# A transformer block over 32 batches: eight batches per turn of the hardware loop instead of four

## The chip, the cores and the metric

One NeuronCore of a Trainium2 chip runs the kernel. The metric is device time in microseconds (us), the median of the runs of one program. Its engines are TensorE (PE; its weight loads are shown as PEld), VectorE (DVE), ScalarE (ACT), GpSimd (POOL) and SyncE (SP), which here issues the transfers. They run their own instruction streams and wait for each other on semaphores.

## The reference

For x of shape 32 x 256 x 128, each batch goes through attention with 16 heads of 8, then two layer norms and a linear layer:

```python
y = layernorm(x, ln_w, ln_b)
q, k, v = y @ wq, y @ wk, y @ wv              # per head, 8 wide
w = softmax(q @ k.T / sqrt(8) + causal)       # 256 x 256, per head
x1 = norm(2 * x + concat(w @ v) @ wo)         # norm: no weights, eps 1e-5
W_eff = W + up_aux @ (lora_up @ (lora_down @ down_aux))
out = norm(x1 + x1 @ W_eff.T + b)
```

All data is float32; the weights are the same for all batches.

## The kernel before

One batch is the unit of work, and all batches are alike. The kernel is a software pipeline over iterations `it` from -4 to 34. An iteration does the parts of several batches at once: stage by stage, the part with offset `o` works on batch `it + o` (offset 4 and 3: statistics of x, normalising, q, k, v and their split into bf16 parts; 2: the transfers that spread the heads, `expand`; 1: row maxima; 0 and -1: scores, exp, masks, weights times v; -1 and -2: output projection and the first norm; -3: linear layer, the last norm and the store). Tiles that live across iterations are rings of 4, so an iteration's tiles are known from its number modulo 4.

Within an iteration the order on each engine is written out by hand in 16 steps `s`. TensorE does up to one unit of row-maxima matmuls (`max_scores`, lines 635 to 640) and one head's scores (lines 652 and 653) in each, with the other matmuls in `side`. VectorE reduces each unit (`row_max`, line 527), with two PSUM banks between the two engines. ScalarE takes the exp of the scores (line 460) and, once per iteration in step 2, copies the transposed maxima into `mT` (line 407); this instruction is a good mark of the iteration. SyncE then writes `mT` into rows of the scores' operand (`qx<-mT`, `max_rows`, line 269), and the first scores of that batch wait for it (line 652). GpSimd masks the exponentials (line 351) and does the small work of the norms. Between engines everything goes by semaphores that only count up; there is no barrier at a turn of the loop.

The instruction stream of each engine is made by `iterate`: iterations -4 to 3 as straight code, a hardware loop over iterations 4 to 23 with four of them in its body (five turns), and iterations 24 to 34 as straight code again. The loop closes with a compare-and-branch on each engine by itself. In the loop the counts that waits compare with are registers, made by `done` through `snap`; in straight code they are constants.

Of the kernel before, what the change touches and what calls it, by code (L numbers as in the profile page):

```python
# [12 lines left out]
BATCHES, SEQ, D = 32, 256, 128  # L13
# [18 lines left out]
RING = 4  # L32
FIRST, LAST = -4, BATCHES + 2
LOOP_FROM = RING
LOOP_TO = LOOP_FROM + (BATCHES - 5 - LOOP_FROM) // RING * RING
RANK, DDIM, UDIM = 4, 100, 50


# [63 lines left out]
def iterate(eng, step):  # L102

    for it in range(FIRST, LOOP_FROM):
        step(Iteration(eng, it, 0, {}))
    with eng.Fori(LOOP_FROM, LOOP_TO - RING + 1, RING) as base:
        cache = {}
        for u in range(RING):
            step(Iteration(eng, base, u, cache))
    for it in range(LOOP_TO, LAST + 1):  # L110
        step(Iteration(eng, it, 0, {}))


def build(nc, x, ln_w, ln_b, wq, wk, wv, wo, w_t, bias, down_t, up_t, down_aux, up_aux_t, out):
    with ExitStack() as ctx:  # L115
# [121 lines left out]
        def _(sp):  # L237
# [34 lines left out]
            def step(it):  # L272
# [19 lines left out]
                if it.runs(3):  # L292
# [3 lines left out]
                    store_parts()  # L296

            iterate(sp, step)
            sp.wait_ge(s_st, 16 * BATCHES)

        @block.gpsimd
        def _(pool):
# [95 lines left out]

            make_masks()
            iterate(pool, step)  # L400

        @block.scalar
        def _(act):
# [60 lines left out]
            for tile, dram in first_weights:  # L464
# [6 lines left out]
                           ACT.Copy).then_inc(s_kmask, 1)  # L471
            act.wait_ge(s_w1, N_W1)
            iterate(act, step)

        @block.vector
# [318 lines left out]
```

## Time and profile before

| | |
|---|---|
| median of 3 runs | 531.74 us |
| the runs | 530.07, 531.74, 531.96 us |
| profiled execution | 532.91 us, of which span 531.1 us |
| mean granted TensorE clock | 0.958 of full speed |
| instructions in the trace | 15,978 |

The span reaches from the first to the last instruction; 1.8 us of the profiled execution lie outside of it. The tables of the profile count only the work of an engine: register, branch and semaphore instructions are left out of busy time and of the counts. "issue" as the end of a wait means that the profile shows nothing that the engine waited for. Queues that the transfer view calls "instruction" carry program code to the engines.

### The profile page before, as it was taken

How to read it: one execution, taken by the hardware profiler on the slowest of the kernel's cores; microseconds unless marked ns; L12 is line 12 of the kernel's file. 1: busy time of each engine (PE TensorE's matmuls, PEld its weight loads, DVE VectorE, ACT ScalarE, POOL GpSimd, SP SyncE). 2: the span in 40 equal slices, each digit the busy share in tenths (PEclk: the TensorE clock that was granted, in tenths of full speed). 3: DMA queues.
4: the chain of work that ended last, by engine and by line, in shares of the span. 5: the costliest groups of instructions: out<-in, count | busy, mean ns of one | idle time of the engine just before them, and what ended most of it. 6: DMA issues, size and time to landing. Idle time of an engine off the chain costs nothing. (4 is left out here: it accounts for less than half of the span.)

```text
span 531.1 us, 15978 instructions
## 1 busy us (share of the span) xinstructions
PE 456.2 (86%) x5512; PEld 333.4 (63%) x5512; DVE 405.9 (76%) x1071; ACT 338.6 (64%) x803; POOL 392.5 (74%) x571
## 2 busy tenths in 40 slices
PE   2467699999899999999999999999999999989861
PEld 1245466767676776676767676676677676666431
DVE  1487778888888888888888888888888888888332
ACT  4212477677776777677767777777767777767620
POOL 6543666888788888888887888888888888866543
PEclk9995799999999999999999999999999999999875
DMA  2554366656655555556665665555555665650000
GB/s 62 139 139 122 87 130 151 162 144 146 157 141 149 145 145 148 138 144 159 160 160 126 156 154 152 138 142 147 147 146 142 162 162 141 128 148 23 23 20 20
DMA packets 70857, 69.11 MB, mean 130 GB/s; under 512 B 6955, under 2 KB 66146, under 8 KB 66146
## 3 DMA queue, kind: packets, MB, share of 16 engines
q1 hardware_dynamic: 70242, 68.48, 52.4%
q8 instruction: 22, 0.36, 0.3%
q10 hardware_dynamic: 576, 0.13, 0.1%
q14 instruction: 17, 0.14, 0.1%
HBM read 47.07 MB, written 20.99 MB: 128 GB/s over the span
## 5 line engine op out<-in xcount | busy, mean ns | idle before, releaser
L527 DVE TENSOR_REDUCE rowmax<-max_bank 128x2 f32<-128x512 f32 (+1 forms) x384 | 253.6, 682 | 46.5 <-PE max_bank L635 31.3
L460 ACT ACTIVATE probs<-score_bank 128x384 f32<-128x384 f32 x512 | 232.1, 491 | 60.0 <-PE score_bank L653 51.3
L351 POOL TENSOR_SCALAR_AFFINE_SELECT probs<-probs 128x1024 f32<-128x1024 f32 x128 | 140.5, 1098 | 40.7 <-ACT probs L460 37.0
L652 PE MATMUL score_bank<-qx,kx 74*128 74x256 bf16 x512 | 133.5, 276 | 5.8 <-DMA qx<-mT 3.5
L639 PE MATMUL max_bank<-kx,qx 128*128 128x128 bf16 x512 | 89.7, 227 | 23.1 <-DVE rowmax L527 21.5
L653 PE MATMUL score_bank<-qx,kx 74*128 74x128 bf16 x512 | 108.7, 220 | 0.0
L668 PE MATMUL pv_bank<-probs,v_ext 128*32 128x256 f32 (+1 forms) x2048 | 105.5, 335 | 2.9 <-POOL probs L351 2.9
L640 PE MATMUL max_bank<-kx,qx 74*128 74x128 bf16 x512 | 89.2, 226 | 0.0
L668 PEld LDWEIGHTS pv_bank<-probs,v_ext 128*32 128x32 f32 x2048 | 55.9, 110 | 42.4 <-issue 17.7
L639 PEld LDWEIGHTS max_bank<-kx,qx 128*128 128x128 bf16 x512 | 48.3, 100 | 51.6 <-DVE rowmax L527 45.1
L338 POOL TENSOR_TENSOR rs<-ve,power 128x2 f32<-128x2 f32 x96 | 69.3, 722 | 8.0
L395 POOL TENSOR_TENSOR parts<-rest,parts 128x512 bf16<-128x512 f32 x32 | 39.6, 1238 | 40.4 <-ACT parts L439 40.4
L635 PE MATMUL max_bank<-kx,qx 128*128 128x128 bf16 x512 | 52.0, 226 | 11.6 <-DVE rowmax L527 6.8
L652 PEld LDWEIGHTS score_bank<-qx,kx 74*128 74x128 bf16 x512 | 50.4, 98 | 14.9 <-ACT probs L460 8.0
L342 POOL TENSOR_SCALAR y<-f,mv,rs 128x128 f32<-128x128 f32 x64 | 51.0, 806 | 8.7 <-POOL rs L338 8.7
L342 POOL TENSOR_SCALAR xhat<-xa,mv,rs 128x128 f32<-128x128 f32 x64 | 51.0, 805 | 8.3 <-POOL rs L338 8.3
L640 PEld LDWEIGHTS max_bank<-kx,qx 74*128 74x128 bf16 x512 | 51.4, 100 | 1.0
L653 PEld LDWEIGHTS score_bank<-qx,kx 74*128 74x128 bf16 x512 | 50.3, 98 | 0.8
L635 PEld LDWEIGHTS max_bank<-kx,qx 128*128 128x128 bf16 x512 | 31.5, 99 | 28.6 <-issue 18.3
L433 ACT ACTIVATE parts<-bank 128x512 bf16<-128x512 f32 x32 | 19.1, 597 | 41.6 <-PE bank L723 41.6
L575 DVE TENSOR_TENSOR rest<-bank,parts 128x512 f32<-128x512 f32 x32 | 22.1, 692 | 28.6 <-ACT parts L433 28.6
L413 ACT ACTIVATE pv_s<-pv_bank 128x256 f32<-128x256 f32 x64 | 24.6, 384 | 26.6 <-PE pv_bank L668 25.3
(76 smaller groups left out, 612.1 us busy)
## 6 DMA issues: line engine op xcount, KB each, us to landing
kx<-k_rows SPq DMA_DIRECT2D x96, 192.0 KB
qx<-q_rows SPq DMA_DIRECT2D x64, 192.0 KB
qx<-q_rows SPq DMA_DIRECT2D x32, 208.0 KB
q_rows<-parts SPq DMA_DIRECT2D x32, 192.0 KB, 2.1
k_rows<-parts SPq DMA_DIRECT2D x32, 192.0 KB, 2.4
xa<-in_x SPq DMA_DIRECT2D x32, 128.0 KB, 5.6
k_rows<-parts SPq DMA_DIRECT2D x32, 128.0 KB, 2.2
xr<-in_x SPq DMA_DIRECT2D x32, 128.0 KB, 6.5
```

The source lines that it names most:

```text
L338: pool.tensor_tensor(rs[:, :], ve[:, :], power[:, :], ALU.pow).then_inc(signal, 1)
L342: ins = pool.tensor_scalar(to[:, n, :], source[:, n, :], mv[:, n, 0:1], rs[:, n:n + 1], ALU.subtract, ALU.mult)
L351: pool.affine_select(out=t, in_=t, compare_op=ALU.is_ge, fill=0.0, base=0, pattern=[[0, GROUP * NB], [1, P]], channel_multiplier=-1)\
L395: pool.tensor_tensor(parts[:, 2, :, :], rest[:, :, :], parts[:, 1, :, :], ALU.subtract).then_inc(s_p3, 1)
L460: act.activation(probs[:, h, 0:PW], score_bank[SCORE_BANK[h]][:, 0:PW], ACT.Exp, scale=SCALE / Q_SCALE)\
L527: dve.tensor_reduce(to, of, AX.X, ALU.max).then_inc(s_mread[unit], 1)
L635: ins = pe.matmul(b[:, g * P:g * P + P], q[:, h, 0:P], k[:, h, 0:P], start=True, stop=True)
L639: pe.matmul(b[:, g * SEQ:g * SEQ + P], q[:, h, P:SEQ], k[:, h, P:SEQ], start=True, stop=True)
L640: ins = pe.matmul(b[:, g * SEQ + P:g * SEQ + SEQ], q[0:SCORE_ROWS, h, P:SEQ], k[0:SCORE_ROWS, h, 0:P], start=True, stop=True)
L652: pe.matmul(b[:, 0:SEQ], k[0:SCORE_ROWS, i, 0:P], q[0:SCORE_ROWS, i, :], start=True, stop=True)
L653: pe.matmul(b[:, SEQ:PW], k[0:SCORE_ROWS, i, P:SEQ], q[0:SCORE_ROWS, i, P:SEQ], start=True, stop=True).then_inc(s_score[h], 1)
L668: ins = pe.matmul(pv_bank[VW * g:VW * g + VW, n * P:SEQ], v_ext[r][:, n, head(h), window], probs[:, h, 0:SEQ] if n == 0 else probs[:, h, S ...
```

## The change

`TURN`, twice the ring, takes the place of `RING` as the loop's step and as the number of iterations in its body. `LOOP_TO` is 4 + 23 // 8 * 8 = 20 instead of 4 + 23 // 4 * 4 = 24. So the loop covers iterations 4 to 19 in two turns of eight, and the straight code behind it iterations 20 to 34. The rings stay at 4 tiles, and nothing changes in what an iteration does or in its order.

```diff
 LOOP_FROM = RING
-LOOP_TO = LOOP_FROM + (BATCHES - 5 - LOOP_FROM) // RING * RING
+TURN = 2 * RING
+LOOP_TO = LOOP_FROM + (BATCHES - 5 - LOOP_FROM) // TURN * TURN
...
     for it in range(FIRST, LOOP_FROM):
         step(Iteration(eng, it, 0, {}))
-    with eng.Fori(LOOP_FROM, LOOP_TO - RING + 1, RING) as base:
+    with eng.Fori(LOOP_FROM, LOOP_TO - TURN + 1, TURN) as base:
         cache = {}
-        for u in range(RING):
+        for u in range(TURN):
             step(Iteration(eng, base, u, cache))
     for it in range(LOOP_TO, LAST + 1):
         step(Iteration(eng, it, 0, {}))
```

## Rows read from the trace of the kernel before

**Rows 1.** The page, part 1: busy us, share of the span, instructions.

```profile
PE 456.2 (86%) x5512; PEld 333.4 (63%) x5512; DVE 405.9 (76%) x1071; ACT 338.6 (64%) x803; POOL 392.5 (74%) x571
```

**Rows 2.** Grouped waits, whole span: us in total, times, longest us.

```profile
ACT probs L460 <- PE score_bank L653: 51.3, 104, 3.6
PEld max_bank L639 <- DVE rowmax L527: 45.1, 98, 1.3
...
DVE rowmax L527 <- PE max_bank L635: 31.3, 38, 1.1
```

**Rows 3.** In order of time, ScalarE, batches 4, 8, 9, 12, 16, 20, 24, 26, 28: start, us.

```profile
106.10 0.37 ACT L407 ACTIVATE mT<-bank 32x256 bf16<-32x256 bf16 x1
...
164.31 0.37 ACT L407 ACTIVATE mT<-bank 32x256 bf16<-32x256 bf16 x1
...
178.59 0.37 ACT L407 ACTIVATE mT<-bank 32x256 bf16<-32x256 bf16 x1
...
221.94 0.37 ACT L407 ACTIVATE mT<-bank 32x256 bf16<-32x256 bf16 x1
...
279.57 0.37 ACT L407 ACTIVATE mT<-bank 32x256 bf16<-32x256 bf16 x1
...
337.20 0.37 ACT L407 ACTIVATE mT<-bank 32x256 bf16<-32x256 bf16 x1
...
394.40 0.37 ACT L407 ACTIVATE mT<-bank 32x256 bf16<-32x256 bf16 x1
...
422.95 0.37 ACT L407 ACTIVATE mT<-bank 32x256 bf16<-32x256 bf16 x1
...
451.65 0.37 ACT L407 ACTIVATE mT<-bank 32x256 bf16<-32x256 bf16 x1
```

**Rows 4.** In order of time: TensorE and VectorE at a turn's boundary, TensorE mid-turn.

```profile
161.11 0.23 PEld L635 LDWEIGHTS max_bank<-kx,qx 128*128 128x128 bf16 x4 [0.38 <-issue]
...
163.24 0.10 PEld L639 LDWEIGHTS max_bank<-kx,qx 128*128 128x128 bf16 x1 [0.89 <-DVE rowmax L527]
...
162.49 0.69 DVE L527 TENSOR_REDUCE rowmax<-max_bank 128x4 f32<-128x512 f32 x1 [0.49 <-issue]
...
204.32 0.23 PEld L635 LDWEIGHTS max_bank<-kx,qx 128*128 128x128 bf16 x4 [0.20 <-issue]
...
206.06 0.10 PEld L639 LDWEIGHTS max_bank<-kx,qx 128*128 128x128 bf16 x1 [0.50 <-DVE rowmax L527]
```

**Rows 5.** Transfer queues (packets, MB, share): 100 to 165, 165 to 390, 390 to 531.

```profile
q8 instruction: 6, 0.10, 0.6%
q14 instruction: 5, 0.04, 0.2%
...
DMA packets 33280, 33.38 MB, mean 148 GB/s; under 512 B 3140, under 2 KB 30944, under 8 KB 30944
## 3 DMA queue, kind: packets, MB, share of 16 engines
q1 hardware_dynamic: 33280, 33.38, 60.6%
...
q8 instruction: 11, 0.18, 0.6%
q14 instruction: 8, 0.07, 0.1%
```

**Rows 6.** Busy time (x instructions) of the loop's second turn, by engine.

```profile
160.30:217.90 57.60, 54.03 (x692) 39.96 (x688) 48.41 (x133) 41.46 (x101) 47.38 (x69) 1.00 0.61 149
```

**Rows 7.** First turn, 135 to 139.5: q8's packet, the landing of qx<-mT, TensorE's wait.

```profile
q8 instruction: 1, 0.02, 1.3%
...
DMA to landing us min/median/max: 1.8/2.7/3.6
...
139.25 0.10 PEld L652 LDWEIGHTS score_bank<-qx,kx 74*128 74x128 bf16 x1 [1.37 <-DMA qx<-mT]
```

**Rows 8.** The page, part 6: transfers, KB each, median us from issue to landing.

```profile
xr<-in_x SPq DMA_DIRECT2D x32, 128.0 KB, 6.5
...
qx<-mT SPq DMA_DIRECT2D x64, 8.0 KB, 1.9
```

## The prediction

> **What bounds the kernel now.** I read the page's busy shares first, then the grouped waits, then the instructions in order of time at one turn boundary, and last the instruction transfers. The reader should see in the shares that no engine is full: TensorE 86% by the modelled matmuls, its weight loads 63%, VectorE 76%, GpSimd 74%, ScalarE 64% [rows 1]. The engines take turns. The waits say it: TensorE waits 45 us for the row maxima of VectorE, VectorE 31 us for the maxima's scores, ScalarE 51 us for scores [rows 2]. So a batch is a chain through several engines, and a delay of any of them can reach the end, less what slack there is.
>
> The period is very regular. Inside a turn of the loop two successive batches are 178.59 - 164.31 = 14.28 us apart. In the straight part behind the loop they are 422.95 - 408.68 = 14.27 us apart. A whole turn of four, with its boundary, takes 279.57 - 221.94 = 57.63 us, and the next 337.20 - 279.57 = 57.63 us [rows 3]. Four batches by themselves are 4 x 14.27 = 57.08 us. So a taken turn boundary costs 0.55 us, and a batch in the loop costs what a batch in straight code costs. At the last turn, where the branch falls through, 394.40 - 337.20 = 57.20 us: 0.12 us.
>
> The 0.55 us can be seen at 160 to 163 us: after the branch TensorE stands 0.38 us for "issue" ahead of its first maxima matmul, where the same place in the middle of a turn shows 0.20; VectorE stands 0.49 us for "issue"; TensorE then waits 0.89 us for VectorE, where it waits 0.50 in the middle of a turn [rows 4].
>
> **The change, part by part.** The operations on data are the same. The loop now covers batches 4 to 19 in two turns of eight, and 20 to 23 move to the straight part.
>
> (a) Boundaries. Before: four taken, one falling through. After: one taken (behind batch 11), one falling through (behind 19). Removed: 3 x 0.55 = 1.65 us. As the boundary shows as lost time in the period itself, nothing hides it, and the whole 1.65 comes off. The batches that move into straight code bring 0, since both kinds take 14.27. The register work ahead of each batch is hidden in either form. Bounds: 1.65 is what rows show; it can't be more than the total of 4 x 0.55 + 0.12 = 2.3 us.
>
> (b) Instructions no longer stay. The instruction transfers tell where code comes from. From 100 to 165 us, the loop's first turn, the queue q8 brings 6 packets (0.10 MB, 16 KB each) and q14 brings 5 of 8 KB. From 165 to 390 us, turns two to five, there is no instruction packet at all. From 390 us on there are 11 and 8 again [rows 5]. So the body of four batches was fetched once and stayed in the engines' instruction memories. TensorE runs 692 matmuls and as many weight loads in a turn [rows 6]; 6 packets of 16 KB over those 1,384 are about 71 bytes each, with its waits and register instructions in the rest, so q8 is TensorE's. After the change its body is twice that: some 2,770 such instructions, 12 packets, 190 KB. Whether this stays, no row shows; the rows show only that some 96 to 112 KB did. I take it that it doesn't: the head of the body has been overwritten when the branch goes back to it, and TensorE stops until its block comes. VectorE and ScalarE also double, and may stop at the same boundary.
>
> The Trainium skill (Advanced Engine Details and Errata, ISA Cache) gives TensorE 128 KB of it, the others 32 KB, in 256-instruction lines. By that page the old body fits, which agrees with the empty stretch of 225 us, and the new one does not. Another of its rules stands with rival 3.
>
> The price of such a stop. One q8 packet is 1.3% of 16 engines in 4.5 us, 0.94 us [rows 7]. From issue to landing the small transfer qx<-mT takes 1.9 us [rows 8]. Request, way and packet together: 1.9 + 1.0 = 2.9 us on TensorE. The trace has one stop of known net price. At 137.9 us TensorE stands 1.37 us for qx<-mT [rows 7], and this first turn takes 164.31 - 106.10 = 58.21 us [rows 3], 0.58 over the others, so some 0.8 us of the stop were absorbed. Net: 2.9 - 0.8 = 2.1 us. VectorE and ScalarE stop in the same microseconds (VectorE's first instruction behind the branch is at 162.5, TensorE's at 161.1 [rows 4]), so their stops lie beside TensorE's and are counted at 0; if VectorE's came after TensorE's, in series, it would cost another 2 to 3 us. Bounds: below, 0 (the block is there after all); above, 6.5 us, the landing of the xr read in this traffic [rows 8], less 0.8, 5.7 us. I take 2.1, near the small transfers, as the block is one packet.
>
> (c) Refetching collides. During the fetches of the first turn one packet of q8 falls into the landing of qx<-mT, the maxima rows that the next scores wait for: it lands after 3.6 us instead of 1.8 [rows 7], and TensorE stands. The small transfer is issued once per batch, a 16 KB fetch comes about every 10 us, so their places shift from batch to batch. The price of four batches with fetches is 0.58 us in the first turn and (451.65 - 394.40) - 57.08 = 0.17 us in batches 24 to 27 [rows 3]. Fetching batches grow by 16: 8 to 11 in the first turn, all eight of the second, 20 to 23 in straight code. The first four of the second turn are the code of the first turn's first four: 0.58. The other twelve at 0.17 per four: 0.51. Sum 1.1 us. Bounds 4 x 0.17 = 0.7 and 4 x 0.58 = 2.3 us.
>
> Sum: -1.65 + 2.1 + 1.1 = +1.55 us. Against the profiled execution's own 532.91 us (span 531.1 and 1.8 around it) this is 534.5. That execution lies 1.2 us above the median of the runs shown, 531.74, so the median to expect is 531.74 + 1.55 = 533.3 us, 0.3% slower.
>
> **The rivals.** A change under 0.5% (2.7 us) can't be told from none here.
>
> Rival 1, the body stays, or its head is fetched ahead in time. For it: no fetch in 225 us of loop, and no limit of the memory is shown. Then (b) is 0 and of (c) only batches 8 to 11 and 20 to 23 pay, 2 x 0.17 = 0.34: -1.65 + 0.34 = -1.3, 530.4 us. Against: twice the code. Chance 0.13.
>
> Rival 2, the other side: the stops come in series. VectorE's head block returns later than TensorE's, or a block just behind the head has gone too and is missed in turn. Two stops of 2.9 less 0.8 are 5.0: -1.65 + 5.0 + 1.1 = +4.45, 536.2 us, 0.8% slower. It decides from a net stop above 2.66 + 1.65 - 1.1 = 3.2 us. For it: VectorE's branch comes over a microsecond behind TensorE's, and the DMA engines are 60% busy. Against: only one boundary is taken, and no other fetch shows as a stop of its own. Chance 0.23.
>
> Rival 3, each taken boundary of the old loop already contains a fetch, so that its price stays as it is. Then (b) is 0 with (c) full: -1.65 + 1.1 = -0.55, 531.2 us. Against it: no instruction packet from 165 to 390 us, with four boundaries taken in the loop, three of them in that stretch [rows 5]. Chance 0.04. It would be the rule of the Trainium skill (Runtime: NRT & Kernel Launch, Instruction fetch mechanics) that a taken branch outside the current two pages always forces a fetch; the trace contradicts it for this loop, whose TensorE body is six packets long.
>
> **How the numbers follow.** My forecast, one stop with most of it net, 530.8 to 534.9 us around 533.3, has 0.60. Rivals 1 to 3 have 0.13, 0.23 and 0.04. The range is 530.5 to 536.3: low end rival 1, high end rival 2; outside it are a stop near the upper bound and noise of the runs (1.9 us between those shown). Slower by over 0.5%: rival 2, 0.23, and a little of the forecast's upper tail, 0.25 together. Faster by over 0.5% would need more than all of the 2.3 us that boundaries cost, and could only come from the spread of runs: 0.03. Within 0.5%: 0.72.
>
> **What the profile after would show.** For (a): batches at 14.27 us, with one excess instead of four. For (b): instruction packets all through the second turn, and behind batch 11 a stand of 2 to 4 us on TensorE put down to "issue", with VectorE's beside it; that batch takes some 17 us instead of 14.88. For (c): packets on q8 growing from 22 to about 34, and now and then a landing of qx<-mT over 3 us with a wait on line 652. The prediction is wrong if the second turn has no instruction packets (rival 1), or if the boundary behind batch 11 costs over 4 us or has a second stop close behind it (rival 2).

## The result and the profile after

The changed kernel takes 535.5 us, the median of 7 runs (534.06 to 536.09), against 531.74 us before (7 runs, 530.07 to 532.67). The ratio is 1.0071, with a 95% interval from 1.0051 to 1.0092: slower, by about 0.7%. The time lies in the predicted range of 530.5 to 536.3, but not where the likeliest case had it (533.3, within 0.5%). Ratios here and below leave out runs more than 1.5% above the fastest of their kernel, which are four of the six of experiment 4 and one of the ten of experiment 10.

In order of time, ScalarE's copy into mT marks batches 4, 8, 11, 12, 13, 14 and 28 (start, us), as in [rows 3]:

```profile
105.99 0.37 ACT L408 ACTIVATE mT<-bank 32x256 bf16<-32x256 bf16 x1
...
163.23 0.37 ACT L408 ACTIVATE mT<-bank 32x256 bf16<-32x256 bf16 x1
...
206.43 0.37 ACT L408 ACTIVATE mT<-bank 32x256 bf16<-32x256 bf16 x1
...
225.36 0.37 ACT L408 ACTIVATE mT<-bank 32x256 bf16<-32x256 bf16 x1 [0.24 <-PE bank L683]
...
241.87 0.37 ACT L408 ACTIVATE mT<-bank 32x256 bf16<-32x256 bf16 x1
...
256.16 0.37 ACT L408 ACTIVATE mT<-bank 32x256 bf16<-32x256 bf16 x1
...
456.83 0.37 ACT L408 ACTIVATE mT<-bank 32x256 bf16<-32x256 bf16 x1
```

Batch 13 to 14 takes 14.29 us, the old period. From 11 to 12, over the only taken boundary, it is 18.93 us, and from 12 to 13 again 16.51 us. Together 35.44 - 2 x 14.27 = 6.90 us for one boundary that used to cost 0.55. The same microseconds in order of time, the first instruction behind the branch on three engines (start, us, and in brackets the idle time before it):

```profile
221.20 0.35 PEld L636 LDWEIGHTS max_bank<-kx,qx 128*128 128x128 bf16 x4 [3.42 <-issue]
...
222.14 0.69 DVE L528 TENSOR_REDUCE rowmax<-max_bank 128x4 f32<-128x512 f32 x1 [3.09 <-PE max_bank L636]
...
222.24 0.49 ACT L461 ACTIVATE probs<-score_bank 128x384 f32<-128x384 f32 x1 [4.04 <-PE score_bank L654]
```

TensorE stands 3.42 us for nothing that the profile shows, where [rows 4] have 0.38. The records of the branch itself say more (engine, operation, duration in ns three times, start). First the kernel before at the same boundary, then the one after, then the code packets from 217.3 to 221.1 us of the one after:

```profile
L106 PEldq COMPARE_BRANCH  x1: 220/220/220, 217.9 to 217.9; - x1
```

```profile
L107 PEldq COMPARE_BRANCH  x1: 3627/3627/3627, 217.3 to 217.3; - x1
...
L107 DVEq COMPARE_BRANCH  x1: 74/74/74, 218.9 to 218.9; - x1
...
L107 ACTq FUSED_REGOPS  x1: 35/35/35, 219.7 to 219.7; - x1
...
L107 DVEq FUSED_REGOPS  x1: 51/51/51, 221.9 to 221.9; - x1
```

```profile
q14 instruction: 3, 0.02, 2.2%
q8 instruction: 1, 0.02, 2.0%
```

The stop is TensorE's branch, which lasts 3.63 us instead of 0.22, and one 16 KB packet of its code moves meanwhile. Before, no code packet moves there. The register operation is the first instruction behind a branch. VectorE's comes at 221.9, three microseconds after its branch, and ScalarE's at 219.7, 2.6 us after its branch at 217.1, where the kernel before has some 0.3 us on each. So these two have a stop of their own beside TensorE's, and TensorE's late matmuls hide its end: when they go on, they have no input yet. The queues of program code (packets, MB, share of 16 engines), 165 to 225 us and 225 to 340 us:

```profile
q8 instruction: 7, 0.11, 0.8%
q14 instruction: 8, 0.07, 0.4%
...
q8 instruction: 11, 0.18, 0.7%
q14 instruction: 5, 0.04, 0.1%
```

There is code traffic all through the second turn, where [rows 5] show none in a loop turn after the first. What the prediction did not have is in the busy time by stretch (us, PE busy and its matmuls, granted clock, DMA share, GB/s):

```profile
210.00:220.00 10.00, 7.70 (x98) 1.00 0.70 178
220.00:230.20 10.20, 8.99 (x65) 0.50 0.32 84
230.20:240.20 10.00, 9.51 (x123) 1.00 0.54 130
```

From late in the stop on, TensorE's granted clock is 0.50, 1.2 GHz, for 10.2 us: it is busy 8.99 us for 65 matmuls, where ten microseconds at 2.4 GHz hold 123.

The books between the two profiled executions. From batch 4 to batch 28 the old one takes 451.65 - 106.10 = 345.55 us [rows 3], which is 3.07 over 24 x 14.27; the new one takes 350.84, 8.36 over. Of the 8.36, 6.90 are the one boundary, 1.46 the falling-through one and the fetches. Of the 3.07, 2.3 are boundaries. So 5.3 us are lost there, and the spans differ by only 3.3 (534.4 against 531.1). The rest is in the drain of the pipeline: behind batch 28 the old execution needs 79.45 us and the new one 77.57. The old one shows a granted clock of 0.51 in one stretch there that the new one has at full speed. First the kernel before, then the one after:

```profile
499.80:503.30 3.50, 3.41 (x25) 0.51 0.02 5
```

```profile
499.80:513.50 13.70, 9.59 (x125) 1.00 0.11 32
```

This part varies from one execution to another of any of these kernels. In all twelve profiled executions the clock stays at half at the very end, from 507 to 533 us on. Six of them have one more stretch at half clock in the drain, with full clock behind it again (before and experiments 2, 3, 7, 9, 10), and need 79.0 to 79.8 us behind batch 28. The six without it (after and experiments 1, 4, 5, 6, 8) need 77.3 to 78.0 us. The medians differ by 3.8 us; how many of the other runs had the stretch is not on record.

### The profile page after: what moved, and what is told of

Read it like the earlier page. It is cut to its first block and busy times, and to the rows that moved or that the text cites. A ratio compares the mean times of both kernels' runs of the same rounds, so it can differ in the third digit from the quotient of the medians.

```text
span 534.4 us, 15820 instructions
## 1 busy us (share of the span) xinstructions
PE 458.9 (86%) x5512; PEld 336.0 (63%) x5512; DVE 406.4 (76%) x1071; ACT 338.1 (63%) x803; POOL 391.4 (73%) x571
## 5 line engine op out<-in xcount | busy, mean ns | idle before, releaser
L640 PE MATMUL max_bank<-kx,qx 128*128 128x128 bf16 x512 | 90.5, 228 | 19.8 <-DVE rowmax L528 17.9
L636 PE MATMUL max_bank<-kx,qx 128*128 128x128 bf16 x512 | 52.7, 228 | 15.5 <-DVE rowmax L528 6.8
```

Of the source, the lines that this page charges most:

```text
L636: ins = pe.matmul(b[:, g * P:g * P + P], q[:, h, 0:P], k[:, h, 0:P], start=True, stop=True)
L640: pe.matmul(b[:, g * SEQ:g * SEQ + P], q[:, h, P:SEQ], k[:, h, P:SEQ], start=True, stop=True)
```

## The experiments

All were timed beside runs of the kernel before on the same chip, which had medians of 530.6 to 531.0 us. Line numbers in their rows are those of the experiment's own file. "Late" is what the two batches over the boundary, 11 to 12 and 12 to 13, take over 2 x 14.28 us in the profiled execution. The kernel before is itself 0.6 us late there (14.88 and 14.28).

**1. The old body, boundaries as after.** Two turns of four, then straight code from batch 12 on.

```diff
-LOOP_TO = LOOP_FROM + (BATCHES - 5 - LOOP_FROM) // RING * RING
+LOOP_TO = LOOP_FROM + 2 * RING
```

> Boundaries as in the changed kernel (one taken, one falling through), but the body keeps four batches; more straight code than in either. Theory 1 (TensorE's head block is gone at the boundary of the body of eight; it stops 3.6 us and its clock falls to half): no stop and no clock drop here, branch 0.25 us as before, three boundaries fewer (-1.65) against up to +1.1 for refetching: 0.5 to 1.5 us faster than before, about 530.5. Theory 2 (the loss is spread over all batches that fetch their code): as in the changed kernel, 2 to 4 us slower than before.

530.16 us, ratio 0.9993 (0.9970 to 1.0015): no different from before. Much more code is fetched here than before and nearly as much as in the changed kernel (39 packets on q8 and 28 on q14, against 22 and 17 before and 46 and 35 after), and nothing is lost. Theory 2, a loss spread over all fetching batches, falls. The expected gain is not resolved in the medians. In the profiled executions, from batch 4 to batch 28, it can be seen: 450.19 - 105.81 = 344.38 us, against 345.55 before.

**2 and 3. The long body on TensorE alone, and on all but TensorE.** Each engine makes its own loop, so the number of batches per turn can differ between them.

```diff
+    turn = 2 * RING if eng.engine == mybir.EngineType.PE else RING       # 2
+    turn = RING if eng.engine == mybir.EngineType.PE else 2 * RING       # 3
+    loop_to = LOOP_FROM + (BATCHES - 5 - LOOP_FROM) // turn * turn
...
-    with eng.Fori(LOOP_FROM, LOOP_TO - RING + 1, RING) as base:
+    with eng.Fori(LOOP_FROM, loop_to - turn + 1, turn) as base:
```

> Only TensorE has the body of eight and two turns; the other engines keep four and five turns. Theory 1: TensorE's branch behind batch 11 again takes some 3.6 us with half clock after it, boundary about 6.9 us, the other engines' own boundaries stay hidden or cost up to 0.5 each: 535 to 537 us. Theory 3 (VectorE's and ScalarE's missing blocks set the stop): near before, within 1.5 us, and no half clock.

> TensorE keeps four batches and five turns, the other four engines have eight. Theory 1: no stop of TensorE at its branches; stops of the others for their 8 KB blocks at most 1 to 2 us once, no half clock: within 1.5 us of before. Theory 3: 3 us or more slower than before.

TensorE alone: 537.43 us, ratio 1.0103 (1.0075 to 1.0131). All but TensorE: 535.42 us, ratio 1.0077 (1.0052 to 1.0101). Either half of the change by itself loses what the whole does. Experiment 2 went as theory 1 had it, 0.4 us above the expected time. Experiment 3 did not: theory 1, with TensorE as the only culprit, is wrong, and theory 3, with the others as the only one, is wrong by experiment 2. The two also show whose queue is whose: from 165 to 390 us experiment 2 has 23 packets on q8 and none on q14, experiment 3 has 17 on q14 and none on q8. The stop of experiment 2 in order of time, then the instructions of experiment 3 at the same place:

```profile
222.03 0.23 PEld L637 LDWEIGHTS max_bank<-kx,qx 128*128 128x128 bf16 x4 [3.74 <-issue]
```

```profile
218.54 0.25 DVE L508 BATCH_NORM_AGGREGATE mv<-st 128x2 f32<-128x6 f32 x2
222.27 1.29 DVE L529 TENSOR_REDUCE rowmax<-max_bank 128x4 f32<-128x512 f32 x2 [3.48 <-issue]
...
219.49 0.87 ACT L462 ACTIVATE probs<-score_bank 128x384 f32<-128x384 f32 x2 [1.56 <-issue]
...
223.02 0.23 PE L641 MATMUL max_bank<-kx,qx 128*128 128x128 bf16 x1 [3.78 <-DVE rowmax L529]
```

In experiment 3 it is VectorE that stands for "issue", 3.48 us, ScalarE 1.56 us, and TensorE's matmuls wait 3.78 us for VectorE (its weight loads 4.00). Its clock falls all the same, though its own body of four stayed and its own branch behind batch 11 took 0.22 us. Experiment 3's busy time by stretch, columns as above:

```profile
219.20:223.00 3.80, 0.04 (x1) 1.00 0.31 86
223.40:226.80 3.40, 3.40 (x31) 0.51 0.03 7
226.80:236.80 10.00, 9.51 (x125) 1.00 0.62 160
```

**4. A prefetch hint for the branch**, on the changed kernel.

```diff
-    with eng.Fori(LOOP_FROM, LOOP_TO - TURN + 1, TURN) as base:
+    with eng.bass.Fori(LOOP_FROM, LOOP_TO - TURN + 1, TURN, engines=[eng.engine], hint_back_edge=True) as base:
```

> The changed kernel with a prefetch hint for the loop-closing branch as the first instruction of each turn. Theory 1: the head block is on hand, TensorE's branch falls from 3.6 us to a few tenths, no half clock behind it; 6.3 us of the boundary come back, 529 to 530 us, 1.5 to 2.5 us faster than before. Theory 2: no faster than the changed kernel, 535. If the hint doesn't reach the block either, the branch stays at 3.6 us.

551.76 us is the median of six runs (541.07 to 554.95). The ratio, 1.0264 (1.0197 to 1.0331), is of two of them alone, 541.07 and 548.98 us: the worst kernel of the study, by an amount that is loosely known. The profiled execution took 554.95 us, so only its stops are read here, not its time. In order of time:

```profile
223.37 0.34 PEld L636 LDWEIGHTS max_bank<-kx,qx 128*128 128x128 bf16 x4 [3.67 <-issue]
...
357.09 0.29 DVE L538 TENSOR_TENSOR attn<-bank,rden 128x128 f32<-128x128 f32 x1 [6.92 <-issue]
...
396.32 0.38 ACT L414 ACTIVATE pv_s<-pv_bank 128x256 f32<-128x256 f32 x1 [6.50 <-issue]
```

TensorE's stop stayed. From 165 to 345 us the queue of the other engines' code is empty, where the changed kernel had 13 packets from 165 to 340. But behind the loop two new stops of 6.9 and 6.5 us appear, on VectorE and ScalarE, in straight code. My expectation was wrong. Why the hint does nothing for TensorE, and why the others then stop twice as long, is open.

**5. No loop at all.**

```diff
-    for it in range(FIRST, LOOP_FROM):
+    for it in range(FIRST, LAST + 1):
         step(Iteration(eng, it, 0, {}))
-    with eng.Fori(LOOP_FROM, LOOP_TO - RING + 1, RING) as base:
...
-    for it in range(LOOP_TO, LAST + 1):
-        step(Iteration(eng, it, 0, {}))
```

> All iterations straight, no boundary at all, every batch fetches its code. Boundaries: -(4 x 0.55 + 0.12) = -2.3 us. Theory 1 (the loss of the changed kernel is the one stop at the taken boundary): no stop, refetching up to +0.1 per batch for 20 batches, so between -2.3 and 0: 528.5 to 530.5 against 530.6 of before. Theory 2 (fetching code costs in itself): slower than before by 1 us or more.

529.5 us, ratio 0.9987 (0.9964 to 1.0009): inside what theory 1 expected, but not told apart from before. From batch 4 to batch 24 it takes 391.48 - 105.52 = 285.96 us, 0.4 over 20 x 14.28, all of it with code being fetched:

```profile
105.52 0.37 ACT L401 ACTIVATE mT<-bank 32x256 bf16<-32x256 bf16 x1
...
391.48 0.37 ACT L401 ACTIVATE mT<-bank 32x256 bf16<-32x256 bf16 x1
```

**6 and 7. Which of the others.** The edit is that of 2 and 3, with VectorE alone, and with GpSimd and SyncE, at eight.

> Only VectorE has the body of eight. Theory 4 (each engine whose doubled body outgrows its instruction memory stops some 3.3 us at the taken branch, and any one of VectorE and TensorE is enough): VectorE's gap behind its branch is 3.3 us as with all four, TensorE starves, its clock falls for a while, batches 11 and 12 take 5 us too much: 534 to 536. If ScalarE or SyncE made the stop: near before.

> Only GpSimd and SyncE have bodies of eight: some 246 and 214 instructions of their own streams, against 368 of VectorE, 322 of ScalarE and 2,878 of TensorE. Theory 4: both bodies stay, no stop, no instruction packets for them in the second turn, within 1 us of before. If every doubled body is lost: a stop of 3 us on GpSimd, 2 to 4 us slower.

VectorE alone: 535.62 us, ratio 1.0086 (1.0056 to 1.0115), the same stop again. GpSimd and SyncE: 529.73 us, ratio 0.9980 (0.9961 to 0.9999), no loss, and from 195 to 345 us, which holds its second turn, no packet of code. Experiment 6 in order of time with the records around VectorE's branch, then all of experiment 7's transfers from 195 to 345 us, where only the data queue moves anything:

```profile
222.41 1.29 DVE L529 TENSOR_REDUCE rowmax<-max_bank 128x4 f32<-128x512 f32 x2 [3.50 <-issue]
...
223.16 0.10 PEld L641 LDWEIGHTS max_bank<-kx,qx 128*128 128x128 bf16 x1 [4.02 <-DVE rowmax L529]
```

```profile
L108 DVEq COMPARE_BRANCH  x1: 74/74/74, 218.8 to 218.8; - x1
...
L108 DVEq FUSED_REGOPS  x1: 51/51/51, 222.1 to 222.1; - x1
```

```profile
DMA packets 22081, 22.36 MB, mean 149 GB/s; under 512 B 2073, under 2 KB 20505, under 8 KB 20505
...
q1 hardware_dynamic: 22081, 22.36, 60.0%
```

Theory 4 holds: each engine's own body decides. All instructions counted, waits and registers too, GpSimd's 246 and SyncE's 214 stay; VectorE's 368 and TensorE's 2,878 don't. ScalarE's 322 stop for 1.56 us in experiment 3, beside VectorE's stop; no run has ScalarE alone at eight, and none has a body length between these, so the limit of no engine is known.

**8 and 9. A stop without a taken branch.** Experiment 1 with a reduction on VectorE that nobody reads, once, ahead of batch 12's first row maximum, in straight code. It adds work and changes no output. The loop's branch falls through just ahead of it, and from 217 to 225 us one 8 KB packet of code moves; both are so in experiment 1 too, which is 0.2 us late (14.45 and 14.28).

```diff
             def step(it):
+                if it.static and it.base == 12:
+                    dve.wait_ge(s_pause, 1)
+                    dve.tensor_reduce(pause_to[:, :], pause[:, :], AX.X, ALU.max)
                 for s in range(HEADS):
```

> The kernel with two turns of four, and in the straight code ahead of batch 12's first row maximum one reduction over 128 x 3072 on VectorE that nobody needs (about 3.3 us). No fetch, no branch there. Theory 5 (a stop costs its length and, because TensorE starves, a stretch at half clock): TensorE waits some 3.5 us for VectorE, its clock falls to 1.2 GHz, batches 11 and 12 take 4.5 to 5.5 us too much: 534.5 to 535.5. If the half clock or the second late batch came with the fetching: 2.5 to 3 us too much and the clock stays: 533.

> As the kernel with the pause of 3.35 us, but the reduction is over 128 x 1536, some 1.75 us. Theory 5: the pause passes to TensorE, less 0.5 to 0.9 us of slack. If the half clock needs the long stop, batches 11 and 12 take only 0.9 to 1.4 us too much and the granted clock stays at 2.4 GHz: 530.5 to 531.5. If any pause of this kind lowers it: 2.5 us or more too much, near 533.

3.35 us of pause: 535.68 us, ratio 1.0109 (1.0076 to 1.0143), as slow as the change. 1.75 us: 533.22 us, ratio 1.0034 (1.0006 to 1.0062). In order of time and by stretch (columns as above), the long pause:

```profile
219.91 3.35 DVE L602 TENSOR_REDUCE pause_to<-pause 128x1 f32<-128x3072 f32 x1
...
223.91 0.10 PEld L645 LDWEIGHTS max_bank<-kx,qx 128*128 128x128 bf16 x1 [3.82 <-DVE rowmax L530]
```

```profile
224.80:228.30 3.50, 3.50 (x33) 0.51 0.16 33
```

and the short one:

```profile
219.22 1.75 DVE L602 TENSOR_REDUCE pause_to<-pause 128x1 f32<-128x1536 f32 x1
...
221.62 0.10 PEld L645 LDWEIGHTS max_bank<-kx,qx 128*128 128x128 bf16 x1 [2.23 <-DVE rowmax L530]
```

```profile
223.50:227.00 3.50, 3.50 (x33) 0.51 0.43 105
```

The stops of TensorE in this table are its idle time in brackets, in experiments 3, 6, 8 and 9 that of its weight loads, with the usual wait for VectorE in it (0.89 us at the old boundary, 0.50 in mid-turn [rows 4]).

| kernel | stop of TensorE, us | clock at half, us | batch 11 to 12 | 12 to 13 | late, us |
|---|---|---|---|---|---|
| before | 1.0 | none | 14.88 | 14.28 | 0.6 |
| 1, two turns of four | 0.5 | none | 14.45 | 14.28 | 0.2 |
| changed | 3.42 | 10.2 | 18.93 | 16.51 | 6.9 |
| 2, TensorE eight | 3.74 | 6.8 | 18.72 | 16.40 | 6.6 |
| 3, all but TensorE | 4.00 | 3.4 | 18.18 | 15.56 | 5.2 |
| 6, VectorE eight | 4.02 | 6.8 | 18.55 | 16.51 | 6.5 |
| 8, pause 3.35 | 3.82 | 3.4 | 17.59 | 15.82 | 4.9 |
| 9, pause 1.75 | 2.23 | 3.4 | 16.00 | 15.68 | 3.1 |

Without a taken branch or missing code at that place the long pause costs what experiment 3's stop does, to 0.3 us. The pauses pass to the batch nearly whole. Against experiment 1, the same kernel without them, they are 17.59 - 14.45 = 3.14 for 3.35, and 16.00 - 14.45 = 1.55 for 1.75. The following batch is then late by 1.5 and 1.4 us, under the lowered clock. The expectation had left open whether the short pause would lower the clock. It did, though the first turn's stop of 1.37 us [rows 7] does not: the granted clock is 1.00 from 139.25 to 149 us. No run holds the clock up through a stop, so that the second late batch is the clock's doing is read from its coming with it each time.

**10. A body of sixteen that runs once.** `TURN = 4 * RING`: no taken branch.

> A body of sixteen batches that runs once: no taken branch, one that falls through behind batch 19, register counts in 16 batches. If the loss is the taken branch to a block that is gone: no stop, as the kernel without a loop, 529 to 530.5. If a long body or its registers cost in themselves: as the changed kernel or slower, 534 and above.

531.17 us, ratio 1.0005 (0.9975 to 1.0034). The longest body of all loses nothing that the interval could show, since nothing jumps back to its head. The way back is what costs, not size or registers. The profiled execution took 537.72 us, and its loss lies elsewhere. Batches 11 to 12 take 14.28 us, but 1 to 2 and 2 to 3 take 17.62 and 16.52, where the kernel before has 14.91 and 14.27. TensorE stood there for a transfer, and its clock fell (grouped waits from 62 to 82 us, then busy time by stretch):

```profile
PEld max_bank L636 <- DMA kx<-k_rows: 3.5, 1, 3.5
```

```profile
77.90:84.70 6.80, 6.58 (x51) 0.50 0.57 154
```

So a third kind of stop, 3.5 us for data, costs much the same: its batch is 2.7 us late, and the following one 2.2 us, under half the clock.

## Why the prediction was half right

**The boundaries (a), -1.65 us.** The profile after shows one taken boundary where there were four. The experiments also show whose 0.55 us it was, at the boundary behind batch 7, which some engines no longer have. With TensorE at five turns and the rest at two (experiment 3), batches 7 to 8 take 14.27 us over TensorE's boundary: nothing. With VectorE alone at eight (experiment 6) they take 14.36, with GpSimd and SyncE at eight (7) 14.93. So nearly all of it was VectorE's branch. As a gain in the median it could not be resolved: the kernels without these boundaries and without a stop (1, 5, 10) came out at ratios of 0.9993, 0.9987 and 1.0005.

**Instructions no longer stay (b).** The mechanism was right, its price was the failed step. The boundary costs 6.90 - 0.55 = 6.35 us more, not 2.1. By the prediction's own sign, a boundary behind batch 11 of over 4 us, its likeliest case was wrong. The sum had three things wrong.

- The stop itself: 3.42 us (3.74 in experiment 2), against 2.9.
- "Some 0.8 us of the stop were absorbed." Experiments 8 and 9 show 0.2 us absorbed of a stop in VectorE's reductions. The stop of 1.37 us that I took the figure from was of another kind: TensorE waited for one operand of the scores while VectorE went on [rows 7]. That this is why it was cheaper is argued, not shown.
- The clock was missing. After a stand of 2.2 to 4.0 us TensorE runs at 1.2 GHz, for 3.4 to 10.2 us. The batch behind is late by 1.3 to 2.2 us. Where the low clock begins early in the stopped batch, that batch is later too (18.93 us in the changed kernel, where it begins 5 us before the mark of batch 12, against 17.59 in experiment 8); that this part is the clock's is argued, not shown. The trace of before had the clock by stretch; I did not ask what a starved TensorE does to it.

"Their stops lie beside TensorE's and are counted at 0" was right in the sum, and says less than it should. VectorE's stop alone (experiment 6) costs 6.5 us, TensorE's alone 6.6, and all together 6.9. They overlap, so removing one of them would have gained 0.3 or 0.4 us.

**Refetching (c).** Expected +1.1 us. Beside the boundary the new execution is 1.46 us over its periods and the old one 3.07 - 4 x 0.55 = 0.87: +0.6. A kernel that fetches everything (experiment 5) is 0.4 over in 20 batches. The price of 0.58 for the first turn's four batches was one batch's, not a rate: 6 to 7 is the late one, 14.74 us before and 14.40 after, and 14.32 to 14.83 in the experiments. (The small transfer goes out twice per batch, x64 [rows 8], not once as the prediction had it.)

The sum now is -1.65 + 6.35 + 0.6 = +5.3, as the traces have it between batch 4 and batch 28. On 531.74 that would be 537.0, outside of the predicted range; on the 530.6 to 531.0 of the experiments' timings of the kernel before it would be 535.9 to 536.3, at its very end. That the median lies in the range is luck: in the two profiled executions the drain gave back 1.9 us, for which neither the prediction nor the change has a reason.

**The rivals.** Rival 1, the body stays, holds for GpSimd and SyncE only. Rival 2 named the right outcome, slower by over 0.5%, and its threshold, a net stop over 3.2 us, was passed; its mechanism, stops in series, is not what happened, for the stops lie side by side and the clock makes the difference. Rival 3 is out: a taken boundary costs 0.55 us where the code stays and 6.9 where it doesn't, and no code packet moves at the old one.

The Trainium skill (Advanced Engine Details and Errata, ISA Cache) gives 128 KB for TensorE, 32 KB for the others, and lines of 16 KB for 256 instructions. As an estimate by that page, TensorE's 2,878 instructions are 180 KiB: too many, which agrees with the run. VectorE's 368 are 23 KiB by the same estimate, less than the 32, and should have stayed; experiment 6 says that they don't. Its packets come in 8 KB, and the blocks that the head and the end of the body share with their neighbours, with one fetched ahead, may be what no longer fits. That is argued, not shown.

## What to carry to other kernels

Count a loop body's instructions per engine, waits and registers too, before lengthening it: a body that stayed in the instruction memory costs about half a microsecond per turn here, one that didn't stay cost 6.9 at its one taken branch, and one engine whose body doesn't stay is enough. Price a stall near TensorE by its length and by what its clock does afterwards; a short dummy operation at the place in question measures both in one run. A difference of 2 us between two profiled executions can come from one stretch at half clock in the drain, so compare stage by stage. Here neither fewer turns nor no loop at all gave a gain that the runs could tell from none.

## What the runs showed of the hardware that was not expected

A pause of 1.75 us in VectorE, which left TensorE standing for 2.23 us, was followed by a granted clock of 0.51 for some 3.4 us. The clock fell even where TensorE's own code was on hand (experiments 3, 6, 8 and 9), and when it waited 3.5 us for a transfer (experiment 10).

A taken branch whose code was gone shows in two ways: TensorE's branch lasted 3.63 us, while VectorE's lasted 0.07 us and its next instruction started 3.3 us behind it (experiment 6).

Packets of code came in 16 KB for TensorE (46 packets, 0.75 MB in the changed kernel) and in 8 KB for the others (13 of them, 0.11 MB, from 165 to 340 us).

With the hint for the loop's branch the changed kernel was 2.6% slower than the one before instead of 0.7%, with stops of 6.9 and 6.5 us in straight code behind the loop.
